# Moving the weight-split pipeline by two slots, halving the resident-weight loads, and normalising batch 0's feed-forward input earlier

## The reference, cut to what matters

```python
def _layernorm(x, axis=-1, eps=1e-05):
    m = jnp.mean(x, axis=axis, keepdims=True)
    v = jnp.var(x, axis=axis, keepdims=True)
    return (x - m) / jnp.sqrt(v + eps)
...
q = _l2norm(q) * jnp.exp(scale)
k = _l2norm(k)
attn = jax.nn.softmax(jnp.einsum('bhid,bhjd->bhij', q, k), axis=-1)
out = jnp.einsum('bhij,bhjd->bhid', attn, v)   # then heads joined, @ w_out + b_out
...
h = silu(x @ w1.T * w1_s) * (x @ w2.T * w2_s)
h = gelu(h @ h1.T * h1_s)                      # exact gelu
h = gelu(h @ h2.T * h2_s)
return h @ w3.T * w3_s
...
x = x + _layernorm(attention(_layernorm(x)))
x = x + _layernorm(feed_forward(_layernorm(x)))
```

## Time and profile before

| | |
|---|---|
| median of 3 runs | 1980.66 us (1978.98 to 1986.99) |
| profiled execution | 1984.11 us, its span 1982.3 us |
| TensorE matmul busy | 1753.8 us, 88% |
| VectorE, ScalarE, GpSimd busy | 62%, 51%, 25% |
| attention slots 0 to 255 | from 46.6 us to 1259.3 us |
| 44 pieces in slots 12 to 187 | from 99.8 us to 948 us |

### The profile page before, as it was taken

How to read it: one execution, slowest core, us unless ns; L and a number is a source line. 1 busy time by engine, 2 the same in 40 slices (tenths; PEclk the granted TensorE clock), 3 DMA queues, 4 the chain that set the end, 5 groups by cost and what they waited for, 6 DMA issues and landing times.

```text
span 1982.3 us, 24990 instructions
## 1 busy us (share of the span) xinstructions
PE 1753.8 (88%) x8576; PEld 1447.4 (73%) x8576; DVE 1222.7 (62%) x2125; ACT 1011.9 (51%) x1349; POOL 503.4 (25%) x590
## 2 busy tenths in 40 slices
PE   4899888989879888889889996689999999999997
PEld 3677667767767777667777875568778787787876
DVE  3687777687677787677677774544544545444453
ACT  2777666767657666656667764423232322313231
POOL 2334434344343444344333331000000000000000
PEclk8999999999999999999999998889999999999999
DMA  3445545545554654545444447220000000000000
GB/s 114 107 119 144 138 120 143 140 125 142 133 130 126 147 141 112 136 120 140 109 105 97 100 101 188 94 92 1 23 2 23 1 23 21 3 22 2 23 2 22
DMA packets 101061, 175.04 MB, mean 88 GB/s; under 512 B 27553, under 2 KB 48289, under 8 KB 99489
## 3 DMA queue, kind: packets, MB, share of 16 engines
q1 hardware_dynamic: 97872, 156.95, 31.4%
q10 hardware_dynamic: 1872, 11.67, 1.9%
q0 software_dynamic: 1152, 4.19, 0.5%
HBM read 56.91 MB, written 31.72 MB: 45 GB/s over the span
## 4 chain that ended last, share of the span: by engine, by line
PE 45%; DMA 18%; issue 14%; DVE 9%; POOL 7%; SPq 3%; ACT 2%; DVEq 0%; POOLq 0%; ACTq 0%
PE pair L1122 12%; PE pair L1123 12%; DMA work<-rows 11%; PE bank L1052 4%; PE bank L994 4%; PE bank L1066 3%; PE pair L1111 2%; POOL rs L401 2%; PE pair L1112 2%; DVE Pl L734 2%; DMA stg<-in_h 2%; DMA rows<-Rp 2%; DMA Dp<-work 2%; DVE work L750 2%; PE bank L1157 2%
## 5 line engine op out<-in xcount | busy, mean ns | idle before, releaser
L1052 PE MATMUL bank<-Ph,V 128*128 128x512 f32 x1024 | 383.0, 415 | 134.8 <-DVE Pl L734 90.9
L528 ACT ACTIVATE P<-pair,sh 128x1024 f32<-128x1024 f32 x256 | 286.4, 1119 | 277.3 <-DVE Pl L734 155.7
L1122 PE MATMUL pair<-hh,f 128*128 128x512 f32 x1024 | 403.6, 394 | 16.3 <-issue 9.2
L1123 PE MATMUL pair<-hl,f 128*128 128x512 f32 x1024 | 402.2, 393 | 0.0
L1052 PEld LDWEIGHTS bank<-Ph,V 128*128 128x128 f32 x1024 | 199.8, 195 | 214.3 <-issue 165.7
L734 DVE TENSOR_TENSOR Pl<-P,Ph 128x1024 fp32r<-128x1024 f32 x256 | 314.6, 1229 | 1.4 <-ACT Ph L533 0.4
L568 ACT ACTIVATE hr<-pair,ct 128x512 f32<-128x512 f32 x128 | 88.3, 690 | 375.9 <-PE pair L1123 375.9
L533 ACT ACTIVATE Ph<-P 128x1024 fp32r<-128x1024 f32 x256 | 271.6, 1061 | 8.1
L1122 PEld LDWEIGHTS pair<-hh,f 128*128 128x128 f32 x1024 | 194.4, 190 | 62.5 <-issue 13.5
L1123 PEld LDWEIGHTS pair<-hl,f 128*128 128x128 f32 x1024 | 194.5, 190 | 40.5
L401 POOL TENSOR_TENSOR rs<-ss,half 128x8 f32<-128x8 f32 x128 | 213.6, 1669 | 10.7
(11 more groups left out here) (100 smaller groups left out, 2896.4 us busy)
## 6 DMA issues: line engine op xcount, KB each, us to landing
stack<-turned SPq DMA_DIRECT2D x128, 384.0 KB, 4.4
stack<-turned SPq DMA_DIRECT2D x128, 256.0 KB, 4.8
work<-rows SPq DMA_DIRECT2D x64, 256.0 KB
high<-sth SPq DMA_DIRECT2D x44, 256.0 KB, 2.5
low<-stg SPq DMA_DIRECT2D x44, 256.0 KB, 2.3
f<-high ACTq DMA_DIRECT2D x11, 1024.0 KB, 5.0
stg<-in_h SPq DMA_DIRECT2D x32, 256.0 KB, 6.9
xt<-in_x SPq DMA_DIRECT2D x8, 512.0 KB, 7.6
```

Source lines behind the costliest of these rows:

```text
L528: e.activation(M.P[:, i % 2, :], M.SB[i % 2][:, :], ACT.Exp, bias=M.sh[:, h:h + 1]).then_inc(S["exp"])
L1052: d = e.matmul(M.OB[:, :], v, p[:, u % 3, j * 512:(j + 1) * 512], start=jt == 0 and m == 0, stop=jt == 3 and m == 2)
L1122: e.matmul(ps, f[:, k, ms], M.hh[src][:, k, :], start=k == 0, stop=False)
L1123: d = e.matmul(ps, f[:, k, ms], M.hl[src][:, k, :], start=False, stop=k == KH - 1 and not low)
```

## The change

It has four edits. `piece_at` counts from slot 14, so that loads fall into i % 4 = 2, splits into 3, counts and high stores into 0, low stores and flags into 1 (the flags come in slots 45, 109, 173 and 189, after 43, 107, 171 and 187). The resident-weight loads are cut into parts of 512 KB, one a slot: layer 0 in slots 246 to 249, layer 1 in 250 to 257, layer 2 in 259 to 266, layer 3 in 267 and 268; the rows of a part are 4 KB long in each partition, where they were 8 KB. `load_xv(0)` comes in slot 245 (and waits for the smaller condition `free0`), `norm3` in 247 and 248, `norm_root3` in 249, `norm3b` in 250 and 251, `turn3`, `x3_high` and `x3_low` in 253.

```diff
--- before.py
+++ after.py
@@ -98,7 +98,7 @@
             order += [(("y", 2 * quad_of(i)), i), (("y", 2 * quad_of(i) + 1), i)]
         if b + 1 < B and i % 32 in (20, 21):
             order.append((("x", 2 * (b + 1) + i % 32 - 20), i))
-        if i == NU:
+        if i == NU - 3:
             order += [(("x3", 0), i), (("x3", 1), i)]
     order += [(("x3", n), SLOTS + n) for n in range(2, 2 * B)]
     plan, last, free = {}, {}, {0: -3, 1: -3, 2: -3}
@@ -172,7 +172,7 @@
 
 FIRST = {0: 0, 1: 8, 2: 24, 3: 40}
 COUNT = {0: 8, 1: 16, 2: 16, 3: 4}
-LOADS = {0: 2, 1: 4, 2: 4, 3: 1}
+LOADS = {0: 4, 1: 8, 2: 8, 3: 2}
 PIECES = 44
 
 
@@ -182,7 +182,7 @@
 
 def piece_at(i, step):
 
-    n, r = divmod(i - 12, 4)
+    n, r = divmod(i - 14, 4)
     return n if r == step and 0 <= n < PIECES else None
 
 
@@ -283,7 +283,7 @@
         if b >= 2:
             q.wait_ge(f"store{b % 2}", 16 * (b // 2))
         q.wait_ge("x1", 16 * (b + 1))
-        free1(q)
+        free0(q)
         e.dma_start(M.xv[:, b % 2, :, :], M.x1[b]).then_inc(S[f"x1{b % 2}"], 16)
 
     def load_low(b, n, ms):
@@ -354,7 +354,7 @@
             store_high(piece_at(i, 2))
         if piece_at(i, 3) is not None:
             store_low(piece_at(i, 3))
-        if i == NU - 7:
+        if i == NU - 11:
             load_xv(0)
         if HEAD <= i < HEAD + 7:
             load_low(0, 0, MS[i - HEAD])
@@ -457,7 +457,7 @@
         n = piece_at(i, 3)
         if n is not None and n + 1 == FIRST[layer_of(n)] + COUNT[layer_of(n)]:
             flag(layer_of(n))
-        if i == NU - 3:
+        if i == NU - 7:
             norm_root3(0)
     for b in range(B):
         for n in range(3):
@@ -612,15 +612,15 @@
             for m in MS[i - HEAD]:
                 gate(0, 0, m)
                 high0(0, m)
-        if i in (NU - 10, NU - 9):
+        if NU - 10 <= i < NU - 6:
             load_f(0, i - NU + 10)
-        if NU - 8 <= i < NU - 4:
-            load_f(1, i - NU + 8)
-        if NU + 3 <= i < NU + 7:
+        if NU - 6 <= i < NU + 2:
+            load_f(1, i - NU + 6)
+        if NU + 3 <= i < NU + 11:
             load_f(2, i - NU - 3)
-        if i == NU + 9:
-            load_f(3, 0)
-        if i == NU:
+        if i in (NU + 11, NU + 12):
+            load_f(3, i - NU - 11)
+        if i == NU - 3:
             x3_high(0)
     for b in range(B):
         for n in range(3):
@@ -932,13 +932,13 @@
                 halves(0, 0, m)
         if piece_at(i, 2) is not None:
             count_piece(piece_at(i, 2))
-        if i in (NU - 5, NU - 4):
-            norm3(0, 2 * (i - NU + 5))
-            norm3(0, 2 * (i - NU + 5) + 1)
-        if i in (NU - 2, NU - 1):
-            norm3b(0, 2 * (i - NU + 2))
-            norm3b(0, 2 * (i - NU + 2) + 1)
-        if i == NU:
+        if i in (NU - 9, NU - 8):
+            norm3(0, 2 * (i - NU + 9))
+            norm3(0, 2 * (i - NU + 9) + 1)
+        if i in (NU - 6, NU - 5):
+            norm3b(0, 2 * (i - NU + 6))
+            norm3b(0, 2 * (i - NU + 6) + 1)
+        if i == NU - 3:
             x3_low(0)
     for b in range(B):
         for n in range(3):
@@ -1345,10 +1345,9 @@
             M.pieces += [(w[:, k, h], high[:, k, h], low[:, 4 * i:4 * i + 4, k, :])
                          for k in range(KH) for i, h in enumerate(halves)]
         M.pieces += [(w3[:, k:k + 2, :], M.hi5[:, k:k + 2, :], M.low5[:, k:k + 2, :]) for k in range(0, KH, 2)]
-        M.loads = [[(M.f1[:, :, :], M.hi12[:, 0:2, :]), (M.f2[:, :, :], M.hi12[:, 2:4, :])]]
-        M.loads += [[(f[:, k:k + 2, :], high[:, k:k + 2, :]) for k in range(0, KH, 2)]
-                    for f, high in ((M.f3, M.hi3), (M.f4, M.hi4))]
-        M.loads.append([(M.f5[:, :, :], M.hi5)])
+        M.loads = [[(f[:, k, :], M.hi12[:, 2 * j + k, :]) for j, f in enumerate((M.f1, M.f2)) for k in range(2)]]
+        M.loads += [[(f[:, k, :], high[:, k, :]) for k in range(KH)] for f, high in ((M.f3, M.hi3), (M.f4, M.hi4))]
+        M.loads.append([(M.f5[:, k:k + 4, :], M.hi5[:, k:k + 4, :]) for k in (0, 4)])
         with nc.Block() as block:
             @block.sync
             def _(e):
```

## The result

The changed kernel took 2009.89 us (median of 4 runs, 2006.99 to 2026.0) and the kernel before, on the same chip, 1979.82 us (4 runs, 1978.29 to 1986.99): a ratio of 1.0161, interval 1.0101 to 1.0222. It is slower by 30 us, where 30 us less were forecast; the measured time also lies outside the forecast's range of 1925 to 1980 us. The profiled execution took 2012.55 us, 2010.7 of them span, 28.4 more than the 1982.3 of before.

What follows compares the result with a forecast made beforehand. The prediction took TensorE to be held in attention by VectorE's waits for split pieces, and at its end by broadcasts behind busy DMA engines. Pieces -35, flags +17 and tail -12 summed to -30 us, so 1951 us, range 1925 to 1980.

Steps and rivals of the forecast that it cites:

- The flags: Flags moved from slot i % 8 = 3 to 5: GpSimd's silences delay roots and TensorE, +17 us, bounds nothing to +25.
- the silence back to the ordinary code: GpSimd after a flag, before the first root: code brought in anew, some 5.9 us in the sum for slot 173.
- The pieces: Pieces two slots on during attention: VectorE's waits ahead of the count go, -35 us net, between 0 and -68.
- the 8 us of counts hidden under V tiles: VectorE's counts near places where it waits for ScalarE: 8 of their 30 us newly hidden, bounds none and all.
- the 4 us for the broadcast: Low store no longer on SP's queue just ahead of the broadcast `normal` waits for: 4 us gained, from 0 to 12.
- rival (c): Low store behind stack transfers delays the load, so slot 4's count, `p_low` and TensorE wait: 1990 to 2010 us, chance 0.14.
- The tail: End of attention, four steps of `normal`: spread loads cut excess from 26 to 14 us, -12 us, bounds 0 and -26.
- the 5 us taken for the first step of `normal`: First step at attention's end: excess from 1 to 1.5 MB ahead of a broadcast, 4 to 6 us, `xv` included.
- a slot that waits issues none: End of attention: each slot issues 0.5 MB, a stalled one nothing, so a broadcast finds only 1 to 1.5 MB before it.
- Rival (a): End of attention: loads are transfer-bound, halving them changes nothing; with half the pieces' gain about 1981 us; family's chance 0.2.
- shorter rows would bring the term near -20 us: End of attention: 4 KB rows halve each queue turn's take from SP, nearer -20 than -12 us; not in the sum.
- The wait before L790: Sign of being right: VectorE's wait ahead of the count falls from 48.8 to under 15 us.

Runs made afterwards that it cites:

- experiment 1: The kernel before with only the pieces, and with them their flags, two slots on: 2024.26 us, 1.0218 of the kernel before.
- experiment 3: The changed kernel with each flag six slots later, in slots 51, 115, 179 and 195: 1977.86 us, 0.9977 of the kernel before.
- experiment 4: The kernel before with only its flags two slots later (45, 109, 173, 189), pieces where they were: 2027.59 us, 1.0236.
- experiment 6: The kernel before with one flag sum for all four layers (slot 187) in place of four: 1968.77 us, 0.9943.
- experiment 7: The changed kernel with one flag sum for all layers, in slot 195, all other edits kept: 1964.45 us, 0.9925 of the kernel before.
- experiment 5: Experiment 3 with the low store issued on SP ahead of that slot's stack transfers: 1958.18 us, 0.9883 of the kernel before.
- experiment 10: Experiment 5 with the one flag of experiment 7: 1945.45 us, 0.9801 of the kernel before.
- experiment 2: The changed kernel with the pieces and flags back in their old slots, so the tail's edits alone: 1984.36 us, 1.0024 of the kernel before.
- experiment 8: The kernel before with each 1 MB load issued as two of 512 KB in the same slot, rows of 4 KB: 1979.40 us, 0.9990.
- experiment 9: Experiment 3 with layer 1's eight loads in slots 258 to 265, layer 2's in 266 and 267: 1978.34 us, 0.9980 of the kernel before.

## Why the prediction was wrong

**The flags: right in place and mechanism, mis-sized by 20 us.** Forecast +17, measured +37. I had read both silences and that the second would no longer be separated from the root. The step that failed is the silence back to the ordinary code. I took 5.9 us for it where my own rows had 7.10 and 7.57, because I ascribed it to the same cause as the 5.94 ahead. It measured 6.95, 8.22, 9.88 and 11.20 us, 36.3 in all where four times 5.9 are 23.6. That is 12.7 of the missing 20 us; where the rest lies is not shown. From the end of the third cast to TensorE's tile I worked out 896.6 - 878.69 = 17.9 us; it took 912.20 - 889.48 = 22.7 us, against 893.18 - 878.69 = 14.5 before. That is 8.2 us for this flag where I took 4, and its block of four slots grew by 10.0; the lower granted clock behind the wait (0.50 where it was 0.79) is one thing that the sum had no term for, but how much of the difference it makes is not shown. Even the upper bound of 25 lay below, since it counted only the silence ahead and the flag itself. Experiments 1, 3 and 4 show that this term alone carries the sign of the result. The trace's 5.96 us ahead of the flag also agree with the Trainium skill ("GPSIMD Engine Reference", Instruction dispatch), which has about 6 us for loading a library kernel's code at its first call. In the kernel before the four returns sum to 29.4 us. The return was 6.8 to 7.7 us wherever a cast ran between the flag and the next other operation (before and in experiment 3), and mostly longer where none did: 6.95 to 11.20 here, 7.16 to 10.48 in experiment 4. Why is not shown.

**The pieces: the wait went, the gain didn't.** Forecast -35 net, measured -7 in the profile outside the flags and 4 us in experiments 6 and 7. The step that failed is the row of reciprocals (`store_rec`) behind a load that has to wait: the sum had no price for it, and it cost about 20 us. The old waits did go (48.8 to 9.3 us, the lines say so), but three other things came with it. First, time that the count had taken came back as waits elsewhere on VectorE: in front of `normal` (25.3 to 40.4 us), of the reciprocal (2.3 to 18.4 us with both of its releasers) and of `head_scale` (10.3 to 36.5 us outside the flag blocks). The slots seem bound by the chain sums, reciprocal, row, broadcast, `normal`; I should have asked what `normal` waits for when VectorE comes to it earlier. Second, the 8 us of counts hidden under V tiles and the 4 us for the broadcast are nowhere in the total: the V waits did shrink by 22 us, but that too is time which came back elsewhere, and the row is now stored behind a load that waits. Third, rival (c)'s place was real and its victim was another: the low store, issued behind the stack transfers, landed in 5.1 us and the load waited for it 43 times, but the count did not suffer, as the load itself took 3.0 instead of 6.9 us. What suffered was `store_rec`, which I had named as queued behind and had not priced. Experiment 5 prices that at 20 us, and with it repaired the pieces gave 23 to 28 us (experiments 6 and 10), so the -35 was not far off but for this term. Net of all, 4 us are left in the change as it stands (experiments 6 and 7). That the chain bounds the slots is read from where the waits went; no run shortened the chain alone, except as far as experiment 5 did.

**The tail: mis-sized, -12 forecast, -0.8 in the profile and nothing in experiment 2.** The step that failed is the 5 us taken for the first step of `normal`, and behind it the argument that "a slot that waits issues none". By the prediction's own terms (18 us for the first step, 14.5 for the others) the first measured 31.6 - 18 = 13.6 us of excess, and the three later ones 11.8 where 9 were taken: 25.4 in all against 26 before. The 6 MB of layers 0 and 1 stand beside the four steps whether they are issued in six slots or in twelve, and the wait went from slot 249 to slots 253 and 257. The load of `xv` had been put inside the 5 us. It is issued just ahead of the sums of slot 246, on SP's queue:

```profile
1235.51 1.45 SPq L287 DMA_DIRECT2D xv<-x  x1
1237.01 1.46 SPq L246 DMA_DIRECT2D Dp<-work  x1
```

These are the place and the length (over 30 us) that the prediction had named as a sign of being wrong; what `xv` alone costs there was not run. Rival (a) describes this part. The rule of the Trainium skill that the engines alternate between queues packet by packet ("DMA: Bandwidth & Descriptors", Queues, rings and completion order) is not shown by any run here. What I drew from it, that shorter rows would bring the term near -20 us, isn't borne out: in experiment 8, 4 KB rows (3456 packets where there were 1872) left the wait at 18.80 us against 18.38. That page's other section, Issuing engines are not separate DMA queues, by which all queues share the same 16 engines, agrees with both experiment 2 and experiment 9, in which only fewer bytes beside the steps made them shorter.

**The sum.** Forecast -35 + 17 - 12 = -30 us. The profiled execution has -7 up to slot 200 outside the flags, +37 for the flags, -0.8 for the tail and -1 behind it, +28.4 in all. The time, 2010 us, is that of rival (c), but by luck: (c) held a count for it, and most of the loss comes from the flags. Pieces (28 us short), flags (20) and tail (11) were all off to the same side.

**Checks named ahead.** The wait before L790 came under 15 us: right. 24 slots in 107 to 111 us: one of two (109.1 and 113.9). Two silences around each flag with TensorE idle 4 to 9 us: two silences, 13 us. No wait of `normal` over 8 us and 75 us for four steps: wrong, 12.64 and 86.9. First step not above 30 us: wrong, 31.6. A count in slot 4 that waits for the load (c): 9.3 us in all, so no.

## What to carry to other kernels

A wait that disappears is a gain only if what comes next isn't itself waiting: ask what the freed engine will then stand in front of, and price everything that is queued behind a DMA issue that has to wait, not only the data it brings. An operation with a silence of GpSimd on both sides of it, as PARTITION_ALL_REDUCE here, costs on both; put it where the engine is idle ahead and behind, and do it as seldom as possible (one sum instead of four was worth 10 to 13 us here). In a queue whose order is written by hand, issue the transfer that others wait for first: that was worth 20 us, with no transfer landing faster. Spreading a transfer over more slots of the same bounded stretch gave nothing here (experiment 2). Taking 3.5 MB out of it shortened the stretch by 10 us (experiment 9), but no gain in the total was measured.

## What the runs showed of the hardware

- GpSimd's PARTITION_ALL_REDUCE is preceded by a silence of 5.7 to 6.0 us (before and changed kernel, eight cases; 9.3 in experiment 3's slot 51, where GpSimd had no other work), and followed by one of 7 to 11 us before the next tensor operation other than a cast (7.06 to 7.66 before; 6.95 to 11.20 after; 6.83 in experiment 3). A cast behind it runs at once.
- A load of 256 KB into SBUF lands in 3.0 us in the changed kernel's places and in 6.9 in those of before, with a broadcast of 256 KB issued ahead of it on the same queue. A store of 256 KB lands in 5.1 us in the slots of the stack transfers, issued behind them or (experiment 5) ahead of them, and in 2.3 us in slots without them.
- Rows of 8 KB or 4 KB made no difference to how long another queue's broadcast had to wait (18.38 and 18.80 us).
- A stall of TensorE is mostly followed by slower matmuls. TensorE, changed kernel, slot 60 (start, length, idle before):

```profile
347.98 0.47 PE L1052 MATMUL bank<-Ph,V 128*128 128x512 f32 x1 [3.54 <-DVE Pl L734]
...
349.60 0.42 PE L1066 MATMUL bank<-oh,nh 128*128 128x256 f32 x1
349.81 0.42 PE L1066 MATMUL bank<-oh,nl 128*128 128x256 f32 x1
...
353.59 0.28 PE L1066 MATMUL bank<-oh,nl 128*128 128x256 f32 x1
353.71 0.28 PE L1066 MATMUL bank<-ol,nh 128*128 128x256 f32 x1
```

The same product starts every 0.21 us at first and every 0.12 us later; the granted clock from 349.6 to 352.5 us is 0.50 (the level of 1.2 GHz), that from 352.8 to 353.8 us 1.00 (2.4 GHz). Of TensorE's 23 waits of more than 2.5 us between 46 and 1290 us of this execution, 20 were followed by such a stretch at 0.50, all but one of those over 3 us among them. A stall thus mostly costs more than its own length.
